# Normalization shift moved from VectorE to GpSimd with new orders of work, and a halved last output projection

## What is computed

```python
h = jnp.maximum(_layernorm(x, axis=-1), 0.0)          # x: (64, 128, 384)
q, k, v = _heads(h @ Wq + bq), _heads(h @ Wk + bk), _heads(h @ Wv + bv)   # 6 heads of 64
scores = jnp.einsum('bhqd,bhkd->bhqk', q, k) / np.sqrt(HEAD_SIZE)
probs = jax.nn.softmax(scores + jnp.where(graph_mask, 0.0, NEG)[:, None], axis=-1)
ctx = jnp.einsum('bhqk,bhkd->bhqd', probs, v)
x = x + ctx @ Wf + bf
```

## Time and profile before

| | |
|---|---|
| time, median of 3 runs | 470.89 us |
| lowest and highest run | 469.98 and 471.25 us |
| the profiled execution's own time | 470.06 us |
| its span, first to last instruction | 468.1 us |
| PE busy | 455.7 us, 97% of the span |
| DVE, ACT, POOL busy | 372.0, 364.4, 305.9 us |
| granted clock of TensorE | full in all 40 slices |

### The profile page before, as it was taken

One profiled execution on the slowest core, in us unless ns is written; L12 is line 12 of the kernel. 1 busy time (PEld: TensorE's weight loads), 2 busy tenths in 40 slices (PEclk: granted clock), 3 DMA queues, 4 the chain that ended last, 5 costly groups with the idle time before them and its releaser, 6 DMA issues.

```text
span 468.1 us, 12797 instructions
## 1 busy us (share of the span) xinstructions
PE 455.7 (97%) x4449; PEld 272.0 (58%) x4450; DVE 372.0 (79%) x740; ACT 364.4 (78%) x822; POOL 305.9 (65%) x308
## 2 busy tenths in 40 slices
PE   6989999999999999999999999999999999999996
PEld 2754656565565655656565565656556565555664
DVE  5999988878886886968688696886969687786964
ACT  5779899976979698795968969587796685996760
POOL 4279487875767857576684857747674866464682
PEclk9999999999999999999999999999999999999999
DMA  8256669999995979969597695967999875796996
GB/s 295 71 100 132 128 131 173 215 198 184 204 198 118 194 174 148 213 145 221 117 210 168 146 221 122 216 157 136 188 157 195 154 156 129 138 147 156 173 176 211
DMA packets 219614, 78.55 MB, mean 168 GB/s; under 512 B 199472, under 2 KB 219568, under 8 KB 219568
## 3 DMA queue, kind: packets, MB, share of 16 engines
q1 hardware_dynamic: 209200, 65.63, 72.1%
q10 hardware_dynamic: 10368, 12.33, 9.5%
HBM read 16.19 MB, written 12.58 MB: 61 GB/s over the span
## 4 chain that ended last, share of the span: by engine, by line
PE 84%; ACT 4%; DMA 3%; DVE 3%; issue 2%; SPq 2%; POOL 1%; ACTq 0%; DVEq 0%; POOLq 0%
PE ps L1068 26%; PE ps L1069 26%; PE ps L1070 26%; PE ps L1130 6%; ACT masked L791 1%; DMA w_raw<-in_Wk 1%; SPq L613 1%; DMA ht_parts<-h_pairs 1%; DVE masked L918 1%; DMA ct_parts<-ctx_parts 1%; ACT qkt_hi L777 1%; ACT h_sb L768 1%; ACT h_pairs L766 1%; POOL h_pairs L678 0%; POOL probs_parts L693 0%
## 5 line engine op out<-in xcount | busy, mean ns | idle before, releaser
L693 POOL TENSOR_TENSOR probs_parts<-masked,probs_parts 128x768 f16<-128x768 f32 x64 | 105.0, 1648 | 54.5 <-ACT probs_parts L806 54.3
L791 ACT ACTIVATE masked<-masked,neg_max 128x128 f32<-128x128 f32 x384 | 118.7, 391 | 19.7 <-DVE neg_max L927 18.5
L1068 PE MATMUL ps<-ht_parts,w_hi 128*128 128x512 f16 (+1 forms) x315 | 111.8, 361 | 1.4 <-DMA ht_parts<-h_pairs 1.0
L1070 PE MATMUL ps<-ht_parts,w_lo 128*128 128x512 f16 (+1 forms) x315 | 111.9, 361 | 0.0
L1069 PE MATMUL ps<-ht_parts,w_hi 128*128 128x512 f16 (+1 forms) x315 | 111.9, 361 | 0.0
L899 DVE SCALAR_TENSOR_TENSOR qkt_lo<-ps,bias_qk,qkt_hi 128x512 f16<-128x512 f32 x96 | 68.6, 742 | 13.9 <-ACT qkt_hi L777 13.8
L699 POOL TENSOR_TENSOR ctx_parts<-ctx_sb,ctx_parts 128x384 f16<-128x384 f32 x62 | 56.8, 921 | 33.5 <-ACT ctx_parts L812 33.0
L688 POOL TENSOR_TENSOR x_bf<-x_sb,b_out 128x384 f32<-128x384 f32 x64 | 63.2, 999 | 23.0 <-DVE y_sb L950 22.9
L777 ACT ACTIVATE qkt_hi<-ps,bias_qk 128x512 f16<-128x512 f32 x96 | 62.8, 677 | 13.1 <-PE ps L1070 13.0
L918 DVE SCALAR_TENSOR_TENSOR masked<-ps,score_unscale,mask 128x384 f32<-128x384 f32 x128 | 70.9, 609 | 1.3 <-PE ps L1130 1.3
L678 POOL TENSOR_TENSOR h_pairs<-h_sb,h_pairs 128x384 f16<-128x384 f32 x60 | 56.5, 949 | 15.1 <-ACT h_sb L768 14.8
(11 more groups left out here) (92 smaller groups left out, 902.5 us busy)
## 6 DMA issues: line engine op xcount, KB each, us to landing
x_sb<-in_x ACTq DMA_DIRECT2D x56, 192.0 KB, 2.8
y<-y_sb SPq DMA_DIRECT2D x56, 192.0 KB, 2.6
x_sb<-in_x SPq DMA_DIRECT2D x8, 192.0 KB, 5.7
y<-x_bf SPq DMA_DIRECT2D x8, 192.0 KB, 3.3
pt_parts<-probs_parts SPq DMA_TRANSPOSE x64, 4.1
ct_parts<-ctx_parts SPq DMA_TRANSPOSE x62, 3.0
adj_sb<-in_adj ACTq DMA_DIRECT2D x14, 64.0 KB, 2.4
w_raw<-in_Wk SPq DMA_DIRECT2D x1, 576.0 KB, 6.4
```

The source lines that it names most:

```text
L693: nc.gpsimd.tensor_tensor(probs_parts[b][:, 1, :], probs[b], probs_parts[b][:, 0, :], ALU.subtract).then_inc(probs_split, 1)
L791: last = nc.scalar.activation(masked[b][:, u, :], masked[b][:, u, :], ACT.Exp, bias=neg_max[b][:, u:u + 1])
L1068: nc.tensor.matmul(to, a_hi, b_hi, start=first, stop=False)
L1070: return nc.tensor.matmul(to, a_lo, b_hi, start=False, stop=last)
```

## The change

1. `shift` is taken from DVE. POOL's `inverse` now issues four instructions instead of two: `neg_mean` = mean x -1 (no wait behind `moments_ready`), epsilon, the power, and `shift_by` = neg_mean x rstd. Two waits of POOL on its own results are added. A memset of `minus_one` comes to the preamble.
2. `finish` and `store` of the last graph (g15, b 3) and its `project_out` work in two halves of 192 columns. The second half goes to the bank of graph 0's output, so that DVE reads the first while PE writes the second; PE waits in addition for `finish` of g15, b 0.
3. The turns of most groups are written anew. The list behind the diff shows what stands differently, in the stages that the prediction speaks of.

```diff
             def inverse(group, item, i):
+                par = group % 2
                 pool.wait_ge(moments_ready, parted(group, i))
+                if group == 1:
+                    pool.wait_ge(consts_set, 7)
+                nc.gpsimd.tensor_tensor(neg_mean[:], moments[par][:, :, 0], minus_one[:], ALU.mult)\
+                    .then_inc(mean_negated, 1)
                 inverse_deviation(group, slice(0, B), i)
                 pool.wait_ge(var_eps_ready, parted(group, i))
                 if group >= 2:
                     wait_normed(pool, group - 2, B - 1, i)
                 inverse_root(group, slice(0, B), i)
+                pool.wait_ge(mean_negated, nth(1, group - 1, 0, i))
+                pool.wait_ge(rstd_ready, parted(group, i))
+                nc.gpsimd.tensor_tensor(shift_by[par][:], neg_mean[:], rstd[par][:], ALU.mult)\
+                    .then_inc(shift_ready, 1)
...
-            def shift(group, item, i):
-                dve.wait_ge(rstd_ready, parted(group, i))
-                if group >= 3:
-                    dve.wait_ge(h_ready, nth(B, group - 3, B - 1, i))
-                shift_graphs(group % 2, slice(0, B))
...
+                if last_of_all(g, b):
+                    for half, columns in enumerate(OUTPUT_HALVES):
+                        dve.wait_ge(y_projected, nth(B, g, b, i) + half)
+                        nc.vector.scalar_tensor_tensor(out=output(g, b)[:, columns], in0=last_half(half),
+                                                       scalar=y_unscale[:, 0:1], in1=x_bf[g % 2][:, b, columns],
+                                                       op0=ALU.mult, op1=ALU.add).then_inc(y_ready, 1)
+                    return
...
+                if last_of_all(g, b):
+                    pe.wait_ge(y_ready, nth(B, g, LAST_HALF_AFTER, i))
+                    for half, columns in enumerate(OUTPUT_HALVES):
+                        for c in range(C):
+                            last = three_passes(last_half(half), ct_parts[b % 2][:, c, :], ct_parts[b % 2][:, C + c, :],
+                                                w_hi[3][:, c, columns], w_lo[3][:, c, columns], c == 0, c == C - 1)
+                        last.then_inc(y_projected, 1)
+                    return
```

More of the change, by code:

```diff
@@ L57 @@
     0: {
[L58 to L68, removed]
@@ new lines @@
+        "aggregate": (28600,), "additive_mask": (28930,), "qk_lo": (28950, 28980, 28990, 29040, 29050, 29060),
+        "values_lo": (28920, 29070, 29170, 29210), "mask_scores": (29090, 29100, 29140, 29160),
+        "largest_score": (29120, 29130, 29190, 29200), "normalize_ctx": (29300, 29430, 29460, 29520),
+        "finish": (29550, 29580, 29700, 29710), "qk_hi": (28840, 28890, 28920, 28970, 28980, 28990),
+        "normalize": (28630, 28640, 28680, 28710), "values_hi": (28860, 29010, 29080, 29160),
@@ new lines @@
+        "aggregate": (18900,), "additive_mask": (18940,), "qk_lo": (19220, 19230, 19240, 19270, 19280, 19290),
+        "values_lo": (19320, 19330, 19540, 19630), "mask_scores": (19340, 19350, 19410, 19420),
+        "largest_score": (19360, 19370, 19440, 19450), "normalize_ctx": (19590, 19650, 19760, 19890),
+        "finish": (19860, 19880, 19990, 20050), "qk_hi": (19130, 19140, 19220, 19230, 19240, 19250),
+        "normalize": (18930, 18940, 18950, 18960), "load_mask": (18660,), "values_hi": (19310, 19320, 19520, 19630),
@@ new lines @@
+        "statistics": (8960, 8970, 9010, 9020), "aggregate": (9080,), "additive_mask": (9260,),
+        "qk_lo": (9530, 9560, 9570, 9600, 9610, 9640), "values_lo": (9660, 9740, 9790, 9840),
+        "mask_scores": (9670, 9680, 9730, 9800), "largest_score": (9690, 9720, 9820, 9850),
+        "normalize_ctx": (9900, 10000, 10140, 10180), "qk_hi": (9410, 9450, 9560, 9570, 9620, 9640),
+        "normalize": (9180, 9190, 9200, 9210), "load_mask": (9060,), "values_hi": (9650, 9700, 9740, 9770),
+        "load": (8810, 8850, 8870, 8900), "exponentials": (9680, 9730, 9810, 9960),
@@ L167 @@
[L167 to L171 removed]
+        "project_v": (40, 60, 70, 80), "weigh_values": (160, 190, 290, 350), "project_out": (310, 380, 410, 450),
@@ new lines @@
+        "values_lo": (50, 90, 130, 150), "mask_scores": (10, 30, 40, 70), "largest_score": (20, 80, 110, 160),
+        "normalize_ctx": (210, 280, 400, 510), "finish": (460, 560, 600, 660), "values_hi": (10, 50, 80, 90),
+        "exponentials": (20, 60, 210, 260), "probs_hi": (100, 110, 230, 330), "ctx_hi": (250, 270, 410, 490),
+        "residual": (-9930, -9910, 0, 10), "probs_lo": (40, 50, 140, 190), "ctx_lo": (150, 160, 230, 280),
+        "transpose_probs": (30, 40, 120, 140), "transpose_ctx": (110, 130, 190, 220), "store": (250, 260, 280, 300),
@@ L202 @@
+        "transpose_ctx": (-19590, -19580, -19520, -19510), "store": (-19480, -19400, -19380, -19370),
     },
     13: {
[L204 to L208 removed]
```

326 lines of the change are left out of this document (162 added, 164 removed).

## The result

| | before | after |
|---|---|---|
| median (lowest to highest), 6 runs each | 470.57 us (469.87 to 472.05) | 465.27 us (465.02 to 467.61) |
| ratio, 95% interval | | 0.9897 (0.9873 to 0.9922) |
| profiled execution, span | 470.06, 468.1 us | 467.61, 465.6 us |
| PE, DVE, POOL busy | | 457.8, 361.9, 309.2 us |

The kernel became 5.3 us faster, 1.1%. The forecast was 468.5 with a range down to 466.4, so the sign was right and the gain was more than twice what I had summed.

The account below looks back on a forecast made before the run. PE, busy 97%, bounds the kernel from 57 to 409 us, DVE the start. Terms 1.2 + 0.7 + 0.3 + 0.3 - 0.5 = 2.0 us took 470.06 to 468.1, median 468.5, range 466.4 to 471.6.

Parts of the forecast that it names:

- the start: Up to 57 us, where DVE sets the pace: shorter PE waits gain 1.2 us in all, between -0.3 and 2.3.
- The end: PE's wait for `ct_parts` of g15 0: `probs_lo` g15 1 comes earlier, gain 0.3 us, bounds -0.7 and 1.2.
- scores of g14: PE's wait ahead of these scores, 1.2 us from start to start, shrinks to 0.5: gain 0.7, bounds -1.0 and 1.2.
- Loop: Groups g4 to g9 change by 0: POOL's added work, about 0.6 us a group, hides; 27.76 us a group stays.
- (b): PE's wait for scale 3 at 26.4 us: DVE loses a 0.9 shift, gains a 0.74 `qk_lo`; 0.2 us earlier.
- (c): PE's wait for `ht_parts` at 37.01 us: later loads of x leave its DMA alone; gain 0.9, bounds 0 and 1.0.
- late aggregate: On DVE, `aggregate` g15 stands behind more work and ends at 398.0 us against 392.7, leaving PE a 0.5 us wait.
- The two masks: On DVE ahead of the g15 aggregate, beside `probs_lo` g13 0: could cost 1.6 us each, delaying it another 1.1.
- Halves: Last graph's output in two halves: shorter last `finish` 0.2 and store landing 0.1, matmuls 0; gain 0.3 us.
- New waits: Costs of the new orders: 0.3 us at `weigh_values` g13 2 and 3, 0.2 for other orders of g10 to g15.
- All stalls close: Rival, chance 0.13: the g14 wait closes whole, `ht_parts` and `ct_parts` gains reach their upper ends; 4.2 us, 466.3.
- Slower: Rival, chance 0.12: the aggregate of g15 delays ACT, PE waits 3.0 us instead of 1.2 at g14; 472.7 us.

Follow-up runs that it names:

- halves alone: Kernel before with only the last output projection, finish and store in two halves: median 469.81 us, ratio 0.9995.
- shift g15: Kernel before with the shift on GpSimd for group 15 alone, orders of work of before: median 467.77 us, ratio 0.9971.
- before with more filling: Kernel before with five filling matmuls instead of one ahead of TensorE's wait at 7 to 9 us: median 469.43 us, ratio 0.9983.

## Why the prediction was wrong, by its own steps

The measured gain was 5.3 us where the sum was 2.0. The step that failed is the stage sum for the start, 1.2, which measured 2.8: the term was mis-sized by 1.6 us. The end (0.3, measured 1.0) and the scores of g14 (0.7, measured 1.2) were too small as well.

- **Loop.** Right. A group still takes 27.76 us with PE full, and POOL's new instructions cost nothing there.
- **The start, 1.2 forecast, 2.8 measured with old orders.** The measured 2.8 is until the scores of g1. (b), 0.2, took the shift of g1 out (0.9) and let one `qk_lo` in, but it left the instructions behind it as long as they were; they shrank by 1.1 us as they slid out from beside POOL's `bias_terms`. And the 1.59 us of g2 stood in the earlier trace rows but in no stage of the sum: that is 1.15 us between the scores of g0 and g1. (c), 0.9, had a wrong mechanism: the wait for `ht_parts` closes with the loads of x where they were. The last transpose of g1 is issued 1.4 earlier, because ACT and PE ahead of it are, and lands 1.9 faster; what shortens the landing isn't shown. Removing that wait alone would have gained nothing: in the four kernels that keep the shifts of g1 and g2 on DVE at these orders (before, halves alone, shift g15, before with more filling) it is 1.0, 0, 0.3 and 0.2 us, and from the scores of g0 to those of g1 all four take 21.39 to 21.42.
- **Scores of g14, 0.7 forecast, 1.2 measured.** Mechanism right (ACT waited 3.7 us for the shift's place on DVE; the kernel with g15 alone gives the 1.2). The late aggregate was right in kind too, but I had it done at 398.0 and it was at 396.84, and ACT came at 399.98 instead of 402.0. The two masks that I feared took 0.74 together. No wait is left.
- **The end, 0.3 forecast, 1.0 measured.** I had looked at when SP issues the transpose and taken its landing as fixed. It is the landing that became shorter, 3.95 to 2.99, by an instruction fetch that no longer falls into it. The bounds, -0.7 to 1.2, held it.
- **Halves, 0.3.** Right as far as can be told: 0.4 to 0.6 at full clock, each time within the scatter; half a `finish` takes 0.42 and the matmuls start 0.082 apart, as worked out.
- **New waits, -0.5.** The new orders cost about 1.3 us in each of two pairs, more than twice the term, and in another place: not `weigh_values` g13 but `values_lo` g2, whose bank PE awaits at 92 to 102 us. The text had named a wait over 0.5 us between 57 and 400 as what would refute it.
- **Rivals.** *All stalls close* came nearest, at 466.3: it had 1.8 for the start, 1.2 for g14 and 0.9 for the landing. I held it at 0.13, since the late aggregate seemed to stand against it. *Slower*, by the same aggregate, didn't come.

What failed as a whole was to read each stall of PE by itself. All of the start hangs on one engine that is full, and time taken from it there is given back more than once, by the instruction itself, by those that no longer lie beside POOL, and by the next stall that they fed.

## What to carry to other kernels

Where one engine is full, price an instruction that is taken from it by its duration in that very place, add the time for which its neighbours are held up beside another engine now and won't be once they slide ahead, and put every such piece into a stage. The move of a 4-column instruction was worth 4 us of 470, a rewritten order of hundreds of items gained nothing and cost about 1; run the small part alone first. And compare executions at the same granted clock, else a difference of 0.4 us is drowned in one of 2.

## What the runs showed of the hardware that I had not expected

- A shift of 128x4 on VectorE, 0.16 us by itself, that began beside a running GpSimd instruction ended 0.02 us after it, in all five such places: it took 0.87 to 1.59 us. Its price is what is left of the other engine's instruction.
- With a fetch of instructions (one packet of the queue q14) within the landing of the last awaited transposing DMA, it takes 3.6 to 4.0 us instead of 3.0. One wait more or less for each group on VectorE moved the fetch by 2.3 us, and the kernel's time by 1.1.
- Four more filling matmuls in a wait of PE at 7 to 9 us kept the clock full in 18 of 18 executions, where 40 of 102 of the kernel before lost 2 us. PE was busy 1.06 of the 2.00 us before 8 us in the trace of before, which kept the clock, and 1.31 in that of after, which lost it; so the trace of one execution doesn't tell whether the next one will.
